# Constant rows set once in Q and K, full products between the first maxima, and ScalarE's copy of the turned attention

## The reference

```
xn   = layernorm(x)
q, k, v = xn @ wq.T + bq, xn @ wk.T + bk, xn @ wv.T + bv    # 16 heads of 8
s    = q @ k.T * 8 ** -0.5;  s = where(xn[:, :, 0] != 0, s, -inf)
att  = softmax(s) @ v @ wo.T + bo
top2 = top_k(xn @ gate, 2);  rank of each token in its expert, kept if < 1280
moe  = sum over kept (expert): weight * (gelu(xn @ c_fc + fcb) @ c_proj + pjb)
out  = x + att + moe
```

## Time and profile before

| | us |
|---|---|
| median of 3 runs | 840.21 |
| lowest and highest | 838.35, 842.05 |
| the profiled execution | 841.55 |
| its span in the trace | 839.7 |
| PE busy | 611.8 |
| DVE busy | 423.4 |
| ACT busy | 398.9 |
| POOL busy | 227.1 |

### The profile page before, as it was taken

How to read it: one execution, slowest core, us unless ns; L and a number is a source line. 1 busy time by engine, 2 the same in 40 slices (tenths; PEclk the granted TensorE clock), 3 DMA queues, 4 the chain that set the end, 5 groups by cost and what they waited for, 6 DMA issues and landing times.

```text
span 839.7 us, 9577 instructions
## 1 busy us (share of the span) xinstructions
PE 611.8 (73%) x3474; PEld 304.9 (36%) x3474; DVE 423.4 (50%) x625; ACT 398.9 (48%) x773; POOL 227.1 (27%) x226
## 2 busy tenths in 40 slices
PE   1674899202299999899999999999899412079985
PEld 0442323000033333584358534863487100023322
DVE  6658855100168888516951686148713201045643
ACT  1532355100157778736784577457745200045561
POOL 5656318777200001100020002000201777730000
PEclk9966557555569999999999999999999655555775
DMA  8898142111011114102321223112312211100011
GB/s 279 245 269 246 78 182 92 54 50 53 22 44 35 52 53 139 34 32 83 113 60 33 70 90 97 32 58 61 111 51 69 76 51 50 47 26 27 2 52 50
DMA packets 61406, 68.56 MB, mean 82 GB/s; under 512 B 8496, under 2 KB 43312, under 8 KB 61360
## 3 DMA queue, kind: packets, MB, share of 16 engines
q1 hardware_dynamic: 54464, 49.86, 20.0%
q0 software_dynamic: 6896, 18.10, 6.4%
HBM read 33.85 MB, written 33.55 MB: 80 GB/s over the span
## 4 chain that ended last, share of the span: by engine, by line
PE 51%; DVE 14%; another core or an unknown queue 11%; ACT 10%; issue 8%; SPq 3%; DMA 2%; DVEq 0%; ACTq 0%
PE bPV L964 15%; PE bX L948 14%; PE bD L1055 9%; DVE nmax L738 8%; ACT probs L596 5%; PE bD L929 4%; ACT hid L623 3%; PE bX L938 2%; SPq L304 2%; PE bD L973 2%; PE bX L1040 1%; PE bX L1044 1%; DMA k_rows<-hid 1%; PE bX L1041 1%
## 5 line engine op out<-in xcount | busy, mean ns | idle before, releaser
L738 DVE TENSOR_REDUCE nmax<-bD 128x2 f32<-128x1024 f32 x256 | 300.2, 1217 | 192.3 <-remote 115.5
L596 ACT ACTIVATE probs<-bX 128x512 f32<-128x512 f32 x512 | 269.1, 597 | 266.4 <-PE bX L948 133.8
L948 PE MATMUL bX<-Q,K 27*128 27x512 f32 x512 | 200.0, 534 | 111.0 <-issue 75.1
L948 PEld LDWEIGHTS bX<-Q,K 27*128 27x128 f32 x512 | 81.4, 209 | 269.4 <-issue 129.8
L929 PE MATMUL bD<-K,Q 25*128 25x512 f32 x512 | 145.1, 544 | 46.1 <-DVE attn L756 28.4
L964 PE MATMUL bPV<-probs,v_aug 128*32 128x512 f32 x1024 | 164.2, 718 | 1.5 <-ACT probs L596 0.7
L500 POOL TENSOR_TENSOR wfc_hi<-wfc,ones 128x512 fp32r<-128x512 f32 x8 | 10.2, 1272 | 359.3 <-DMA pjb<-in_pjb 359.3
L929 PEld LDWEIGHTS bD<-K,Q 25*128 25x128 f32 x512 | 61.8, 213 | 81.4 <-DVE attn L756 35.5
L1055 PE MATMUL bD<-wpj,hid 128*128 128x128 f32 x640 | 74.0, 276 | 7.7 <-DVE xeT_lo L776 4.8
L1055 PEld LDWEIGHTS bD<-wpj,hid 128*128 128x128 f32 x640 | 72.4, 192 | 9.4 <-issue 9.4
L623 ACT ACTIVATE hid<-bX,fcb 128x512 f32<-128x512 f32 (+1 forms) x96 | 55.2, 614 | 27.3 <-PE bX L1044 26.6
(11 more groups left out here) (104 smaller groups left out, 477.7 us busy)
## 6 DMA issues: line engine op xcount, KB each, us to landing
Q<-q_rows SPq DMA_DIRECT2D x32, 256.0 KB, 4.3
K<-k_rows SPq DMA_DIRECT2D x128, 64.0 KB, 3.4
slot_x<-hid POOLq DMA_DIRECT2D x10, 512.0 KB, 2.9
xe<-slot_x SPq DMA_DIRECT2D x8, 640.0 KB, 4.5
slot_y<-ye SPq DMA_DIRECT2D x8, 640.0 KB, 3.9
q_rows<-hid SPq DMA_DIRECT2D x8, 512.0 KB, 4.6
k_rows<-hid SPq DMA_DIRECT2D x8, 512.0 KB, 5.6
acc<-in_x SPq DMA_DIRECT2D x8, 256.0 KB, 8.8
```

What stands on the lines that cost most here:

```text
L596: taken(nc.scalar.activation(probs[:, (g % 2) * 4 + i, :], next_x()[:], ACT.Exp, scale=SCALE))
L738: nc.vector.tensor_reduce(nmax[q][:, k, 2 * pair:2 * pair + 2], bank()[:], AX.X, ALU.max, negate=True).then_inc(s_dd, 1)
L948: filled(nc.tensor.matmul(next_x()[:], K[u][rows_used, QUAD * q + h, j * P:(j + 1) * P], Q[u][rows_used, q, :], start=True, stop=True))
```

## The change

The stacks in HBM lose their constant rows: 24 rows for Q and 25 for K. The tiles Q and K, both 128 x 2 x 512 now, are filled with ones once by GpSimd; loads and maxima write only the rows that vary, by eight DMAs for a quad, one for each head of Q and of K. The scores read K by quad, from the head's strip. In the loop of the first maxima TensorE also makes two products of a 128-row matrix of ones with the 128x512 one-hot table in front of each pair from the third step on (12 pairs), and four more before the first group; nobody reads them. The wait for the ranks' copies, which read that bank, moves ahead of them. The turned attention goes into a bX tile instead of a bD tile, and ScalarE copies it to `attnT` ahead of the last exponential of group 2, instead of VectorE; the projection waits for that copy. At the end of the last batch it is the same. The counts follow.

```diff
--- before.py
+++ after.py
-WR_DMAS, LOAD_DMAS, MAX_DMAS = 4, 5, 4
-ZERO_DMAS, ROW_DMAS = 10, 4
+WR_DMAS, LOAD_DMAS, MAX_DMAS = 4, 8, 4
+ZERO_DMAS = 10
...
-D_TURN = GB * 2 + 4
+D_TURN = GB * 2 + 3
...
-    return 1 + 4 * (n + 1) + (n + 3) // 4 + 2 * HC * NCH * experts_before
+    attn_turned = (n - 2) // GB if n >= 2 else 0
+    return 1 + 4 * (n + 1) + (n + 3) // 4 + attn_turned + 2 * HC * NCH * experts_before
...
-        q_rows = nc.dram_tensor("q_rows", [B, H, STRIP, T], F32, kind="Internal").ap()
-        k_rows = nc.dram_tensor("k_rows", [B, H, STRIP, T], F32, kind="Internal").ap()
+        q_rows = nc.dram_tensor("q_rows", [B, H, ROW_MASK, T], F32, kind="Internal").ap()
+        k_rows = nc.dram_tensor("k_rows", [B, H, ROW_MAX, T], F32, kind="Internal").ap()
...
-        K = [sb(f"K{u}", [P, UH, T], F32R) for u in range(UNITS)]
+        K = [sb(f"K{u}", [P, 2, T], F32R) for u in range(UNITS)]
...
                 if u == 0 and q == 0:
                     sp.wait_ge(s_wr[b], WR_DMAS * 16)
                     sp.wait_ge(s_wm[b % 2], b // 2 * 16 + 16)
-                sp.dma_start(Q[u][:, q, :].bitcast(F32), q_rows[b, h0:h0 + QUAD].rearrange("h r t -> (h r) t")
-                             ).then_inc(s_load[u][q], 16)
                 for h in range(QUAD):
-                    sp.dma_start(K[u][STRIP * h:STRIP * (h + 1), QUAD * q + h, :].bitcast(F32), k_rows[b, h0 + h]
-                                 ).then_inc(s_load[u][q], 16)
+                    for tile, stack, n in ((Q[u], q_rows, ROW_MASK), (K[u], k_rows, ROW_MAX)):
+                        sp.dma_start(tile[STRIP * h:STRIP * h + n, q, :].bitcast(F32), stack[b, h0 + h]
+                                     ).then_inc(s_load[u][q], 16)
...
-            sp.wait_ge(s_rows, ROW_DMAS * 16)
-            sp.wait_ge(s_padded, UNITS)
+            sp.wait_ge(s_ones, 2 * UNITS)
             load_quad(0, 0, 0)
...
-            pool.dma_start(row_ones, tail_d[4:5, 0, :].to_broadcast([P, T])).then_inc(s_ones, 16)
-            nc.gpsimd.memset(row_zeros, 0.0).then_inc(s_fill, 1)
-            pool.wait_ge(s_fill, 1)
-            pool.wait_ge(s_ones, 16)
-            every_q, every_k = (t.rearrange("b h r t -> (b h) r t") for t in (q_rows, k_rows))
-            for stack, r0, r1, src in ((every_q, ROW_MASK, ROW_MAX, row_ones), (every_q, ROW_MAX, STRIP, row_zeros),
-                                       (every_k, ROW_MAX, NR_EXP, row_ones), (every_k, NR_EXP, STRIP, row_zeros)):
-                pool.dma_start(stack[:, r0:r1, :], src[:, None, :].to_broadcast([P, r1 - r0, T])).then_inc(s_rows, 16)
-            for u in range(UNITS):
-                nc.gpsimd.memset(K[u][:].bitcast(F32), 0.0).then_inc(s_padded, 1)
+            for tile in (*Q, *K):
+                nc.gpsimd.memset(tile[:].bitcast(F32), 1.0).then_inc(s_ones, 1)
...
                     if i == 0:
                         wait(act, s_pv, n - 1)
+                    if i == 3 and g == 2 and not first:
+                        take_attnT()
                     taken(nc.scalar.activation(probs[:, (g % 2) * 4 + i, :], next_x()[:], ACT.Exp, scale=SCALE))
+
+            def take_attnT():
+                taken(nc.scalar.copy(attnT[:], next_x()[:]))
...
-            def take_attnT():
-                take()
-                nc.vector.tensor_copy(attnT[:], bank()[:, 0, :]).then_inc(s_dd, 1)
-                d.step()
...
-            def project(since=2):
-                pe.wait_ge(s_dd, d.value(-since))
+            def project(x_since):
+                pe.wait_ge(s_xd, x.value(-x_since))
...
-                turned(lambda k: attn[:, k, :])
+                filled(turned(lambda k: attn[:, k, :], next_x()))
...
+            def keep_clock(n):
+
+                for _ in range(n):
+                    nc.tensor.matmul(bPV[:], ones_r[:], hot_f, start=True, stop=True)
+
             for s in range(1, LEAD):
+                if s == 2:
+                    pe.wait_ge(s_ranks, 1)
                 for pair in range(2):
+                    if s >= 2:
+                        keep_clock(2)
                     scores_for_max(0, 0, s, pair)
                 if s == 5:
                     maxima(0, 0)
-            pe.wait_ge(s_ranks, 1)
+            keep_clock(4)
             for g in range(4):
                 group(0, g, first=True)
```

More of the change, by code:

```diff
@@ L64 @@
 N_CONST, N_LATER = 8, 3
-WR_DMAS, LOAD_DMAS, MAX_DMAS = 4, 5, 4
-ZERO_DMAS, ROW_DMAS = 10, 4
+WR_DMAS, LOAD_DMAS, MAX_DMAS = 4, 8, 4
+ZERO_DMAS = 10
 D_FIRST = (LEAD + 4) * 2
-D_TURN = GB * 2 + 4
+D_TURN = GB * 2 + 3
 D_EXPERTS = 2 * 2 * NCH
-assert D_FIRST % 2 == 0 and D_TURN % 2 == 0 and D_EXPERTS % 2 == 0
 D_EXPERTS_FROM = D_FIRST + EXPERTS_FROM * D_TURN + D_TURN
@@ L161, in build @@
         xT = [ye[:, TT * q:TT * (q + 1), :].rearrange("p n c -> p (n c)") for q in range(2)]
-        row_ones, row_zeros = probs[:, 0, :], probs[:, 1, :]
         scan, rank = (wfc[q][:].rearrange("p (n e) -> p n e", e=E) for q in range(2))
@@ L197, in build @@
         s_fill = sem("s_fill")
-        s_padded = sem("s_padded")
         s_ones = sem("s_ones")
-        s_rows = sem("s_rows")
         s_xin = [sem(f"s_xin{b}") for b in range(B)]
@@ L438, in _ @@
                 nc.gpsimd.memset(v_aug[n][:], 0.0).then_inc(s_fill, 1)
-                pool.wait_ge(s_fill, 2 + 3 * n)
+                pool.wait_ge(s_fill, 1 + 3 * n)
                 for q in range(2):
@@ L480, in _ @@
             nc.gpsimd.memset(hid_f[:, 0:per], 0.0).then_inc(s_fill, 1)
-            pool.wait_ge(s_fill, 8)
+            pool.wait_ge(s_fill, 7)
             pool.wait_ge(s_nq[0], MAX_DMAS * 16)
@@ L600, in fill_v @@
                 if b == 0:
-                    act.wait_ge(s_fill, 7)
+                    act.wait_ge(s_fill, 6)
                 va = v_aug[b % 2][:].rearrange("p j (u r) c -> p (j u) r c", u=UNITS)
@@ L619, in experts @@
                         act.wait_ge(s_d, before + at + 1)
-                        nc.scalar.copy(xeT[0][:, c0:c0 + w], bD[at % 2][:, 0, 0:w]).then_inc(s_xhi, 1)
+                        nc.scalar.copy(xeT[0][:, c0:c0 + w], bD[(before + at) % 2][:, 0, 0:w]).then_inc(s_xhi, 1)
                     for hc in range(HC):
@@ L819, in group @@
                     normalise(1)
-                if g == 2 and not first:
-                    take_attnT()
                 if g == 3 and not first:
@@ L928, in scores_for_max @@
                     rows_used = slice(STRIP * h, STRIP * h + NR_MAX)
-                    last = nc.tensor.matmul(to[:, n, :], Q[u][rows_used, q, k * P:(k + 1) * P], K[u][rows_used, QUAD * q + h, :],
+                    last = nc.tensor.matmul(to[:, n, :], Q[u][rows_used, q, k * P:(k + 1) * P], K[u][rows_used, q, :],
                                             start=True, stop=True)
@@ L947, in scores @@
                 rows_used = slice(STRIP * h, STRIP * h + NR_EXP)
-                filled(nc.tensor.matmul(next_x()[:], K[u][rows_used, QUAD * q + h, j * P:(j + 1) * P], Q[u][rows_used, q, :],
+                filled(nc.tensor.matmul(next_x()[:], K[u][rows_used, q, j * P:(j + 1) * P], Q[u][rows_used, q, :],
                                         start=True, stop=True))
@@ L967, in with_v, with turned @@
                 last.then_inc(s_pv, 1)
-            def turned(src, n=TT):
-                to = free()
+            def turned(src, to, n=TT):
                 for k in range(n):
-                    last = nc.tensor.transpose(to[:, 0, k * P:(k + 1) * P], src(k), ident[:])
-                done(last)
+                    last = nc.tensor.transpose(to[:, k * P:(k + 1) * P], src(k), ident[:])
+                return last
             def output_sums(b, u):
                 pe.wait_ge(s_pvo, b * UNITS + u + 1)
-                turned(lambda k: pv_s[:, k * P:(k + 1) * P])
-            def project(since=2):
-                pe.wait_ge(s_dd, d.value(-since))
+                done(turned(lambda k: pv_s[:, k * P:(k + 1) * P], free()[:, 0, :]))
+            def project(x_since):
+                pe.wait_ge(s_xd, x.value(-x_since))
                 to = free()
@@ L1017, in group @@
                 if g == 3 and not first:
-                    project()
+                    project(4)
                 if g == GROUPS + 1:
@@ L1027, in rows_in @@
                     c0, w = CH[c]
-                    turned(lambda k: xe[:, c0 // P + k, :], w // P)
+                    done(turned(lambda k: xe[:, c0 // P + k, :], free()[:, 0, :], w // P))
                     return d.value()
```

## The result

| | changed | before |
|---|---|---|
| median | 838.91 us (20 runs) | 839.25 us (20 runs) |
| lowest, highest | 823.39, 865.73 | 830.38, 863.69 |
| the profiled execution | 828.99 | 841.55 |
| its span, mean granted clock | 826.8, 0.812 | 839.7, 0.799 |

In the median nothing changed, against 818.5 forecast. The executions of the changed kernel lie in three groups: 5 at 823 to 829, 12 at 836 to 843, 3 at 853 to 866. The ratio of 0.988 (95%: 0.983 to 0.992) uses only executions within 1.5% of each kernel's own fastest, here 5 of 20 of the changed kernel and 15 of 20 of the kernel before, so it sets the best of the one against the usual of the other; over all executions there is no gain. The profiled execution is one of the five, so this trace shows the kernel at its better end, and where the others differ is told by the experiments.

A forecast was written before the change was run, and what follows sets the result against it. DMA was taken to bound the front, TensorE the groups (partly at half clock), GpSimd's indirect DMAs the pauses. Against 841.55 us, -8.5 +1 -15 +1.5 -0.5 = -21.5 gave 820.0, as a median 818.5; range 809 to 835.

The forecast's parts named there:

- The front: Start of the kernel: smaller fills free the normalisations, fewer bytes in the stacks; -8.5 us, bounds -6 and -10.5.
- the front stays: Rival: x loads or stacks give the 8.5 us back; 827 with the clock gained, 840 with neither; chance 0.08.
- The eight loads: SP issues eight DMAs a quad instead of five, 0.46 us each, just hidden before the maxima's DMAs: 0 us.
- the rival of SP's queue: Rival: load DMAs above 0.79 us each delay the maxima's DMAs; 889 at 1.1 us; chance 0.04 including unseen waits.
- The price of the products: First maxima: two products make a pair cost TensorE 1.3 to 1.6 us at half clock; +1 us, bounds 0 and +4.
- the fill doesn't do what it says: Rival: clock stays 0.50 as before and twelve pairs run at the slower pace; 835 us, chance 0.13.
- The gain of the clock: Groups before the first pause run at 2.61 us instead of 4.06; -15 us, given 3 in 4.
- The recovery: Behind the first pause the clock starts low and returns later, at the turn of sums in group 9: +1.5 us.
- late return: Rival: turn of sums in group 9 fails, half clock lasts to batch 2's projection; +12.4 us, 831; chance 0.25.
- enters and leaves the pause five groups further on: GpSimd's 42 us from first maxima to indirect DMAs stays, so TensorE's faster groups before the pause aren't lost in it.
- The turned attention: Its copy moves from VectorE (0.69 us) to ScalarE (0.57); at most 0.2 us a batch either way, taken as -0.5 in all.

The follow-up runs named there:

- rows_only: Kernel before with constant rows, loads and unpadded K alone; no full products, VectorE copies the turned attention: 828.46 us against 839.62, ratio 0.988.
- no_fill: Changed kernel without any full products, in the loop or before the groups: 828.37 us against 839.62; repeated in a launch without pauses, 658.33 against 681.19.
- after_third: The changed kernel itself, unaltered, timed a third time, in a launch without the pauses: 669.97 us (649.21 to 684.27) against 670.27 for the kernel before.
- burst16: Changed kernel with no products in the loop, 16 in one piece ahead of the first group: 829.01 us (820.25 to 863.17), ratio 0.979.
- lead12: Changed kernel with 12 more full products in one piece at the third step of the first maxima: 833.89 us (819.82 to 847.65), ratio 0.979.
- burst10_split: Changed kernel with its products replaced by 10 in one piece before the groups, and GpSimd's addition of bo in eight parts: 826.85 us, ratio 0.976.
- burst_split_again: Second timing of the changed kernel with 16 products in one piece before the groups instead of its own, bo added in eight parts: 848.8 us against 840.62.
- after_again: The changed kernel itself, unaltered, timed once more beside the others: 840.85 us (839.31 to 858.96) against 840.56, ratio 1.000.
- best: burst16_split plus one product in place of each pair of scores that the last eight groups lack: 840.93 us (811.51 to 867.13).
- pause_fill: burst16_split plus 16 products in group 5 of batch 1 and group 11 of batch 6; three times, all without pauses: 654.21, 658.13, 654.32 us.
- burst16_split: burst16 with GpSimd's addition of bo to acc cut into eight parts, one for each batch: first time 829.59 us (814.38 to 838.2), ratio 0.970.

## Why the prediction was wrong

**The front** (-8.5, bounds -6 and -10.5): right in its mechanism, a little small. The fills gave the 8.1 us counted, x came 1.4 earlier, which I had not counted, and up to the first maxima 1.3 more were gained, where I had counted 0.45 for the stacks. In the time it is 11.2 (rows_only), 0.7 outside the bounds; the rival "the front stays" is refuted.

**The eight loads** (0): right. 0.30 us each instead of 0.46; the rival of SP's queue would have needed 0.79.

**The price of the products** (+1, bounds 0 and +4): this step failed. "With two products a pair costs TensorE 1.3 to 1.6 us" does not follow from its own rows. By the earlier trace rows a product takes 0.56 us until the next starts, so two take 1.12, and the pair's 0.79 overlaps them by little: 1.87 measured. Then 12 pairs x (1.87 - 1.14) = 8.8 us, and the four products ahead of the groups, 2.0, count too: 10.8, of which TensorE had some idle before; measured 9.3 (no_fill to changed, 83.14 to 92.48). The rival "the fill doesn't do what it says" used the same +4 and so gave 835; with 9.3 it gives 840.5, and with the measured 11.2 for the front as well 838.3, beside the medians of 838.91 and 840.85. This is a sum and no profile: the two profiles of the changed kernel with the pauses, at 828.99 and 858.96, both lie outside its middle group. GpSimd lost only 4.8 us by it (clear at 88.22 against 83.40 in rows_only), because the four and the last two steps don't stand before its maxima.

**The gain of the clock** (-15, 3 in 4): the second step that failed, in its chance and in what it is set against. Where the clock rose in the loop (after_third) or in a piece (burst16, lead12), groups took 2.6 us from the start and single executions reached 820, the number forecast. But of three profiles of the changed kernel one shows it, so 3 in 4 was too high. And the 15 us were counted from a rise at 136.7 that isn't steady either: without products it came at 121 in no_fill and not before the pause in rows_only, whose medians are equal, and where the piece of burst16 gave full clock from the first group, the best execution was 2.6 us below that of no_fill. I had read the rises at 136.7 and 785.2 as the effect of the 128-row work before them, and the turn of sums at 772.84, which raised nothing, as the exception. Over all the profiles the same instructions are followed by a rise in one execution and not in the next: the projection behind the first pause was in burst10_split (222.58, the rise at 225) and was not in burst_split_again (225.23), where the clock stayed low to 290.5. The Trainium skill (TensorE: Matmul & The Clock Gate, "What's actually happening") says that the number of slow matmuls ahead of the rise differs between runs of one kernel, but puts what that costs at under 1% of a typical span. The first half agrees with what is seen here. The second doesn't: the changed kernel's own executions reach from 823 us at a mean granted clock of 0.819 to 866 at 0.759, which is 5%.

**The recovery** (+1.5) and the rivals on it: the return was early in some profiles and late in others. It came at about 236 in the changed kernel's profile and at 248.6 in after_again, in both behind the turn of the attention and ahead of the projection, which lay behind the pause since the clock had been low in front; at 281.6 in lead12, 289 in best and 290.5 in burst_split_again, past the "late return" (work at half clock from 215 on), each behind a turn of sums. What I had not priced is the second pause. I had left it out as not touched by the change. But 0.50 can last from it to the end, in after_again from 658 on, in best from 655, and that goes with every profile above 845 us. The argument "enters and leaves the pause five groups further on" held in lead12, with full clock from 70 to 135, where it put the projection into the pause; in burst16 and in the kernels with bo in parts, with the clock down at 125 to 128, the projection still came behind the pause (222.58 to 229.92). That its place makes the return late is not shown: burst_split_again had its projection behind the pause and was late too.

**The turned attention** (-0.5): nothing to be seen, 828.46 against 828.37.

What stays open: why the pauses come and go (both kernels, the same chip, other launches), and what decides in which execution the clock rises. Two kernels that beat both are no_fill and, with less scatter, rows_only: 828.4 against 839.62 beside them, and without the pauses 658.33 against 681.19 for no_fill. Single executions of other versions are faster, to 811.51. Of their medians only that of burst10_split is lower, 826.85, with two of six executions at 857.6; without pauses that of pause_fill is, by 4 us.

## What to carry to other kernels

Work that only keeps a clock up is paid in full at low clock before it can earn anything: count it by the start of the next instruction for each of its instructions, beside the pace of the engine that it must not overtake. If it is tried, one piece where the next work follows at once was the surer way here (the clock rose in or right behind every piece in front that was profiled, 10 products in the shortest), but while the pauses lasted no piece gained clearly in the median over leaving the products out (826.85 at best against 828.37). Look at several profiles, and judge by the median over many executions. Large constant fills of padding on GpSimd are worth removing, less for their bytes than for what VectorE can't do meanwhile.

## What was not expected of the hardware

- GpSimd's addition of 128x4096, 8.86 us, held a cast of 128x16 on VectorE for 6.70 us instead of 0.18 (6.80 in after_again), and eight parts cut that to 1.03. The fill of K had held the first normalisations in the same way (9.21 us against 1.11). The Trainium skill (SBUF — State Buffer, "SBUF: two separate sides") says that the port pair which GpSimd shares with some of VectorE's instructions is an exclusive lock, held for the whole instruction of the one that starts first; the trace agrees, the addition starts at 120.06 and the cast, begun at 122.25, ends with it at 128.95. Whether this cast is one of those instructions isn't seen in the trace.
- The same program on the same chip takes 828 or 658 us, with or without two stretches of some 80 us in which TensorE, VectorE and ScalarE nearly stop while GpSimd issues 64 indirect DMAs at 1.27 us each.
- TensorE stood at 1.2 GHz while it was busy 5.0 of 5.0 us with 128-row products and strips (80 to 85 us), and at 2.4 GHz in another execution of the same instructions from 84.3 us.
- The clock fell from 2.4 to 1.2 GHz at 128.4 us in burst16_split, with TensorE busy 4.61 of the 5 us before 128.
